# A gated delta-net block with a routed FFN on one core: output's roots on VectorE, a shorter root for m, v scaled behind x's norm, q transposed by halves, VectorE's loop one step earlier

## What is computed

```
x = x + attn(layernorm(x))
    h  = rms_norm(x);  q, k = l2norm(silu(h Wq)), l2norm(silu(h Wk));  v = silu(h Wv)       # 8 heads of 128
    per token and head:  S = alpha S;  S += k (beta (v - k S));  o = q S / sqrt(128)
    h  = (rms_norm(o) * o_norm_w * silu(h Wg)) Wo;   x = x + h
    m  = rms_norm(x);   y = relu(m W_fc)^2 W_proj;   result x + y
x = x + ffn(layernorm(x))
    logits = x gate_W^T;  pi = 20 sinkhorn rounds;  the two best of 8 experts per token
    y = sum over the two of pi * (silu(x Wgate) * (x Wup)) Wdown
```

## Time and profile before

| | us |
|---|---|
| median of 3 runs (lowest, highest) | 2452.66 (2448.92, 2453.04) |
| the profiled execution, its own time | 2450.82 |
| its span, first to last instruction | 2449.0 |
| busy PE, PEld, DVE, ACT, POOL | 2167.5, 1907.3, 1810.2, 1076.7, 763.9 |

### The profile page before, as it was taken

The page is one execution under the profiler, slowest core; times in us unless marked ns, Lnnn a source line. Parts: engine busy times, 40 slices in busy tenths (PEclk is TensorE's granted clock), DMA queues, the critical chain, the costliest instruction groups (busy, mean ns, idle before and its releaser), DMA issues.

```text
span 2449.0 us, 51704 instructions
## 1 busy us (share of the span) xinstructions
PE 2167.5 (89%) x16283; PEld 1907.3 (78%) x16283; DVE 1810.2 (74%) x4317; ACT 1076.7 (44%) x2288; POOL 763.9 (31%) x1559
## 2 busy tenths in 40 slices
PE   4579999999999999999999998632599999999998
PEld 4468888888888888888888887521599999999887
DVE  6678887888888888888888787377666676666553
ACT  2334444444444444444444443221555555555442
POOL 0113332332333333323323333000234444434332
PEclk9789999999999999999999999855799999999999
DMA  5312212212122122122121221000345445445340
GB/s 189 104 33 48 42 36 48 41 36 52 37 43 48 36 46 42 36 49 41 36 54 35 44 46 25 7 7 2 135 158 175 154 162 182 148 155 175 123 129 18
DMA packets 307850, 182.26 MB, mean 74 GB/s; under 512 B 244716, under 2 KB 286064, under 8 KB 298512
## 3 DMA queue, kind: packets, MB, share of 16 engines
q1 hardware_dynamic: 255184, 149.21, 21.7%
q0 software_dynamic: 11280, 29.31, 4.2%
q10 hardware_dynamic: 41264, 2.51, 1.1%
HBM read 150.23 MB, written 32.51 MB: 75 GB/s over the span
## 4 chain that ended last, share of the span: by engine, by line
PE 43%; DVE 29%; issue 10%; DMA 6%; POOL 5%; ACT 3%; SPq 2%; POOLq 1%; DVEq 1%; ACTq 0%
PE ps_inva L744 9%; PE ps_invb L744 9%; PE ps_back L744 8%; PE ps_back L1984 4%; DMA xi<-xy_d 3%; PE ps_back L2001 3%; DVE state L1661 3%; DVE o_s L1682 2%; PE ps_front L1884 2%; DVE xi L1613 2%; DVE xi L1607 2%; DVE yi L1606 2%; DMA xy_d<-lane_x 2%; DVE yi L1612 1%; PE ps_back L1974 1%
## 5 line engine op out<-in xcount | busy, mean ns | idle before, releaser
L614 DVE TENSOR_TENSOR w_lo<-w_raw,w_hi 128x512 fp32r<-128x512 f32 x288 | 190.1, 688 | 3.9
L744 PE MATMUL ps_back<-w_hi,eh_hi 128*128 128x256 f32 x624 | 180.1, 289 | 3.2 <-DVE eh_lo L624 3.2
L744 PE MATMUL ps_back<-w_lo,eh_hi 128*128 128x256 f32 x624 | 176.5, 283 | 0.0
L744 PE MATMUL ps_back<-w_hi,eh_lo 128*128 128x256 f32 x624 | 176.4, 283 | 0.1
L698 ACT ACTIVATE w_hi<-w_raw 128x512 fp32r<-128x512 f32 x288 | 169.5, 626 | 0.0
L710 ACT ACTIVATE sact<-ps_inva 128x512 f32<-128x512 f32 (+1 forms) x96 | 49.8, 519 | 239.5 <-PE ps_inva L744 213.3
L1940 PE MATMUL ps_back<-state,kqT_t 128*128 128x128 f32 x1024 | 132.7, 282 | 24.0 <-DVE r_s L1641 22.7
L1940 PEld LDWEIGHTS ps_back<-state,kqT_t 128*128 128x128 f32 x1024 | 125.4, 193 | 32.5 <-DVE r_s L1641 26.5
L1283 ACT ACTIVATE v_s<-ps_front 128x512 f32<-128x512 f32 x64 | 38.1, 595 | 230.0 <-PE ps_front L744 230.0
L1283 ACT ACTIVATE g_s<-ps_front 128x512 f32<-128x512 f32 x64 | 38.3, 599 | 226.1 <-PE ps_front L744 214.8
L744 PE MATMUL ps_inva<-xT_hi,w_hi 128*128 128x512 f32 (+1 forms) x384 | 135.5, 353 | 1.9 <-DVE xT_lo L619 1.7
(11 more groups left out here) (385 smaller groups left out, 6743.0 us busy)
## 6 DMA issues: line engine op xcount, KB each, us to landing
w_raw<-L_ffn_W_gate_dram SPq DMA_DIRECT2D x24, 1024.0 KB
w_raw<-L_ffn_W_up_dram SPq DMA_DIRECT2D x24, 1024.0 KB
w_raw<-L_ffn_W_down_dram SPq DMA_DIRECT2D x24, 1024.0 KB
dT<-alphaT_d SPq DMA_DIRECT2D x32, 512.0 KB, 3.7
x_all<-L_attn_x_dram SPq DMA_DIRECT2D x4, 1024.0 KB, 10.0
hTr<-hT_d SPq DMA_DIRECT2D x32, 128.0 KB, 3.7
lt_d<-aP SPq DMA_DIRECT2D x256, 8.0 KB, 1.5
xi<-low_d SPq DMA_DIRECT2D x32, 128.0 KB
```

The lines of the kernel that those rows point to most:

```text
L614: V.tensor_tensor(piece(w_lo[p], m).bitcast(F32R), piece(w_raw, m), piece(w_hi[p], m), ALU.subtract).then_inc(split[n], 1)
L744: ins = MM(out_, w[a].bitcast(F32R), x[b].bitcast(F32R), start=start and n == 0, stop=stop and n == 2)
```

## The change

- **o's root**: POOL keeps three operations (`o_squares`) and writes the value into `root_v[:, 1, :]`, signalled by `ov_ready`. DVE's `k_root` puts k's value into `root_v[:, 0, :]`, waits for `ov_ready`, and takes both roots in the same ten instructions, 128x16 instead of 128x8. `tail_o` then runs from inside `k_root`, ahead of sqk, nb1 and nbh, which come after it. In step 31, which has no front, DVE takes o's root by itself.
- **m's root**: the mean and epsilon are folded into the sum of squares (scale and start value of L1693), and the last factor into m's scaling on DVE (L1699, now with a second, constant factor). POOL's chain has 7 operations instead of 9. x's root keeps its 9.
- **v**: POOL waits for `xf_ready` of tile t-1 ahead of `scaled_v`.
- **q**: PE does the first half of `state_q`, the transposes of q's first half, the second half, the transposes of the second half.
- **DVE's loop** holds steps 1 to 28.
- The memsets of ones and state and the first semaphore counts move from POOL to DVE, at the start; the last tile's code loses one operation.

```diff
-                roots(os_[:, 1, :], or_[:, 0, :], or_[:, 1, :], o_pool, n + 3, or_ready)
+                pool.tensor_tensor(root_v[:, 1, :], os_[:, 1, :], qe[:, :], ALU.add).then_inc(ov_ready, 1)
...
-                n = N_ROW * t + 1
-                link(pool.tensor_scalar(mrow_v[:, 1:2], mrow_v[:, 0:1], 1.0 / D, RMS_EPS, ALU.mult, ALU.add), m_pool, n)
-                row_root(mrow_v[:, 1:2], mrow_r[:, 0:1], mrow_r[:, 1:2], m_pool, n, mr_ready)
+                newton(mrow_v[:, 0:1], mrow_r[:, 0:1], mrow_r[:, 1:2], m_pool, N_M * t).then_inc(mr_ready, 1)
...
                 if tail:
                     x_root(t - 1)
+                    if more:
+                        pool.wait_ge(xf_ready, t)
                 if more:
                     scaled_v(f)
...
-            def k_root(f, q):
+            def k_root(f, q, t=None):
...
+                    dve.wait_ge(ov_ready, t + 1)
+                    dve.sem_inc(dve_turn, 1)
+                    root(ch, root_v[:, :, :], root_r[:, :, :], root_a[:, :, :])
+                    tail_o(t)
+                rk = root_r[:, 0, :]
+                ch.mark(V.tensor_tensor(sqk[:, :], root_v[:, 0, :], rk, ALU.mult))
...
-            step(1, 1, True, True, True)
-            with dve.Fori(1, PAIRS) as i:
+            with dve.Fori(0, PAIRS - 1) as i:
                 for p in range(2):
-                    step(2 * i + p, p, True, True, True)
+                    step(2 * i + p + 1, 1 - p, True, True, True)
+            step(TILES - 3, 1, True, True, True)
...
-                state_q(t)
-                if more:
-                    transposes(f, FU_TQ, q_s)
+                for g in range(G):
+                    state_q(t, [g])
+                    if more:
+                        transposes(f, FU_TQ, q_s, [g])
```

More of the change, by code:

```diff
@@ L148, in program @@
         msc = sb("msc", [P, 2])
-        ssk, nv, na, rn, sqk, nb1, dbh = (sb(n, [P, H]) for n in ("ssk", "nv", "na", "rn", "sqk", "nb1", "dbh"))
+        ssk, sqk, nb1, dbh = (sb(n, [P, H]) for n in ("ssk", "sqk", "nb1", "dbh"))
+        root_v, root_r, root_a = (sb(n, [P, 2, H]) for n in ("root_v", "root_r", "root_a"))
         nbh = sb("nbh", [P, 2, H])
@@ L1147, in first_root, with newton @@
                 link(pool.tensor_scalar(r.bitcast(I32), v.bitcast(I32), -0.5, ROOT_MAGIC, ALU.mult, ALU.add), chain, n)
[L1149 to L1162, removed]
+            def newton(v, r, a, chain, n):
                 first_root(v, r, chain, n + 1)
@@ L1168, in row_root @@
                     link(pool.tensor_scalar(a, r, r, v, ALU.mult, ALU.mult), chain, m + 1)
-                    link(pool.tensor_scalar(r, a, -3.0 * c * c, r, ALU.add, ALU.mult), chain, m + 2)
+                    last = pool.tensor_scalar(r, a, -3.0 * c * c, r, ALU.add, ALU.mult)
+                    if k < 2:
+                        link(last, chain, m + 2)
                     c *= -2.0 * c * c
-                pool.tensor_scalar(r, r, 1.0 / c, None, ALU.mult).then_inc(ready, 1)
+                assert c == NEWTON
+                return last
             def front_scalars_free(f):
@@ L1494, in aggregate @@
                 return ins
+            V.memset(ones[:, :], 1.0).then_inc(consts, 1)
+            V.memset(state[:, :], 0.0).then_inc(consts, 1)
+            for s in front_evac + back_evac:
+                dve.sem_inc(s, 1)
+            dve.sem_inc(ba_ready, 2)
+            dve.sem_inc(pre_tr, 4)
+            for s in [x1_stored, xf_stored] + hT_stored:
+                dve.sem_inc(s, 16)
             for n in range(XPARTS):
@@ L1737, in step @@
                 if more:
-                    k_root(f, q)
-                if tail:
+                    k_root(f, q, t - 1 if tail else None)
+                elif tail:
+                    ch = Chain(dve, o_dve)
+                    dve.wait_ge(ov_ready, t)
+                    dve.sem_inc(dve_turn, 1)
+                    root(ch, root_v[:, 1, :], root_r[:, 1, :], root_a[:, 1, :])
                     tail_o(t - 1)
@@ L1806, in _ @@
             dve.wait_ge(mv_ready, TILES)
[L1807 to L1808 removed]
+            root(ch, mrow_v[:, 0:1], mrow_r[:, 0:1], mrow_r[:, 1:2])
             dve.sem_inc(mr_ready, 1)
[L1810 removed]
+            tail_m(TILES - 1, 1.0)
             tail_fc(TILES - 1)
@@ L1870, in project, with transposes @@
                 last.then_inc(filled, 1)
-            def transposes(f, u0, src):
-                for n in range(G):
+            def transposes(f, u0, src, halves=range(G)):
+                for n in halves:
                     ps, filled = front_bank(f, u0 + n)
@@ L1945, in state_k, with state_q @@
                     heads(t, BU_KS + g, g, lambda c: kqT[:, c, 0, :], lambda c: cols(state, c))
-            def state_q(t):
-                for g in range(G):
+            def state_q(t, halves=range(G)):
+                for g in halves:
                     heads(t, BU_QS + g, g, lambda c: kqT[:, c, 1, :], lambda c: cols(state, c))
```

52 lines of the change are left out of this document (20 added, 32 removed).

## The result

The changed kernel takes **2387.9 us** (median of 4 runs, 2386.5 to 2388.1), the kernel before 2452.85 (2448.9 to 2456.1). The ratio is 0.9735, with a 95% interval of 0.9718 to 0.9752. The profiled execution took 2388.1 us, with a span of 2386.3.

A forecast was written before the change was run, and what follows sets the result against it. PE's busy time was taken as the bound, its idle time as what can be won. Savings of 2.07 us a pair, 29.0 in 14 pairs, 32.2 with the ends, off 2450.8 gave 2418 us, range 2404 to 2434.

The forecast's parts named there:

- the one on the loop: DVE's jump moves from ahead of even steps to ahead of odd ones; no change in its 1.73 us cost taken.
- The 1.73: DVE's issue wait after its loop jump, between os and ssk: 1.73 us, bounds 1.73 either way.
- Rival 4: At the loop jump: DVE's instructions come later because four other engines fetch then; 2442 to 2467 us, chance 0.05.
- where I had 3.2: Start and end of the kernel, outside the 14 pairs: 3.2 us won together, mostly at step 31 and step 29.
- The 0.55: DVE's copy L1614 beside POOL's v: held 0.55 us, leaving 0.36 of the 0.91 won at x's norm.
- Rival 1: DVE's copy L1614 beside POOL's v isn't held: 0.91 instead of 0.36 reaches r_s, 2411 us, chance 0.32.
- POOL wasn't first: Case behind x's norm: v's scaling gets ahead of L1612, DVE held 2.2 us, 2459 us, chance 0.06.
- x's blocks are not what PE waits for next: Case at the small inverse: x's blocks from DRAM (margin 0.6) hold PE, 2432 us, chance 0.14.
- the 0.75 that I had for the end: Step 31, where DVE waits 2.75 us for o's root: its replacement ends about 0.75 us sooner.
- The 0.30: PE's wait for m's scaled rows: 0.30 us a step goes, as m's root comes 0.74 earlier.
- the sum 0.42 meets the 0.41 that DVE is earlier: Step 16: PE's waits for kqT (0.25) and o's rows (0.17) go together; 0.41 us taken.
- A step can't fall much below 42.9: Floor of a step from PE's busy time, 42.89 us; only PE's idle time, 3.67 us a pair, can be won.

The follow-up runs named there:

- e12: The kernel before with 35 empty semaphore increments ahead of DVE's first wait, loop still over steps 2 to 29: 2429.35 us, ratio 0.9901.
- e3: The kernel before with 163 empty semaphore increments ahead of DVE's first wait, loop still over steps 2 to 29: 2429.75 us, ratio 0.9908.
- e4: The changed kernel with 93 empty semaphore increments ahead of DVE's first wait: 2417.0 us, ratio 0.9854.
- e6: The changed kernel with 60 empty semaphore increments ahead of DVE's first wait: 2417.9 us, ratio 0.9848.
- e1: The kernel before with DVE's loop moved to steps 1 to 28 and nothing else: 2503.1 us, ratio 1.0203.
- e2: The changed kernel with DVE's loop moved back over steps 2 to 29: 2436.2 us, ratio 0.9929.
- e7: The changed kernel without POOL's wait for x's norm (`xf_ready`) ahead of v's scaling: 2403.0 us, ratio 0.9783.
- e9: The changed kernel with all of o's root back on POOL (15 operations) and o's scaling behind k's scalars: 2400.4 us, ratio 0.9779.
- e10: The changed kernel with m's root in nine operations on POOL again: 2398.55 us, ratio 0.9780.
- e8: The changed kernel with `state_q` whole ahead of all of q's transposes, as before: 2388.8 us, ratio 0.9735.
- e11: The changed kernel with POOL's v waiting for the pairs' inverse instead of x's norm, `msc` copy moved ahead of x's norm: 2384.3 us, ratio 0.9726.
- e5: The changed kernel with 48 empty semaphore increments ahead of DVE's first wait: 2386.5 us, ratio 0.9727.

## Why the prediction missed, and where it held

**The step that failed is the one on the loop**: "I take no change, as the mechanics of a step are the same for both parities." The 1.73 was read rightly as the price of a jump, but that both parities do the same work says nothing about whether it stays, and no case in the list of rivals took it away. The bound of 1.73 in the kernel's favour, 14 times, would have given 2394, outside the range that I then stated. The price is a property of where the loop's code lies. Moved to steps 1 to 28 in the changed kernel, the loop begins at instruction 333 and touches three pages, and the wait is gone. That is worth some 23 us on the kernel before (e12, e3) and 29 to 30 on the changed one (e4, e6); that it is worth more there because the other parts had used up the slack beside it is argued, not shown. The page showed the clue: q14, 0.76 MB of instructions, for a program whose loop should be fetched once. I hadn't read that row. Rival 4 had the mechanism by its name (instructions that come late) but only in the direction of worse, and e1 shows that side too: 50 us slower. It needs no other engine's jump for it, though: the wait at the jump is about as long where the jumps meet (1.88 to 1.90 us in e1, e4 and e6) as where they don't (1.76 before, 1.96 in e2). What makes e1 slow is the second page, and the clock that falls behind it.

**The rest was right in sum, in part by luck.** With the loop again in four pages (e4, e6) the changed kernel takes 2417.0 and 2417.9, against 2418 forecast, and its pair is 2.0 us shorter than before, against 2.07. But the step without the jump gives 1.27 and 1.13 there, where I had 1.0, and the one with it 0.74 and 0.89, where I had 1.07: two misses that cancel. Without fetching on either side the parts are worth 2429.4 - 2387.9 = 41.5, and undone one by one 15.1 + 12.5 + 10.7 + 0.9 = 39.2: nearly additive. The pairs say the same with less scatter:

| kernel | mean of 13 pairs, us | 14 times the difference from the changed one |
|---|---|---|
| before | 89.75 | 58.7 |
| before, padded 35 | 87.95 | 33.6 |
| changed | 85.55 | |
| v not behind x (e7) | 86.49 | 13.1 |
| o's root on POOL (e9) | 86.18 | 8.7 |
| m's root of nine (e10) | 86.49 | 13.1 |
| q whole (e8) | 85.49 | -0.9 |
| v behind the pairs (e11) | 85.43 | -1.7 |

The four parts make 34.0 of 33.6. The 8 us between that and the 41.5 lie outside the pairs, where I had 3.2.

Single terms:

- *v behind x's norm*: x's norm at 0.41 in every step, v's recorded 2.48, DVE first at the two-input operation, the reductions beside v at 1.22 as ever, the copy held. All as taken, but the copy is held for 0.32 and not for 0.55. The 0.55 was wrong as a sum too: 3.1 - 2.4 + 0.14 - 0.22 + 0.2, as I wrote it, is 0.82, by which v's move would have been worth 0.09 a step and the forecast 2422. In the trace v ends 2.88 behind x's norm, and the copy 0.08 behind v. Rival 1, where it isn't held at all, is refuted; e11 shows that the price reaches PE for a few hundredths a step. The Trainium skill (SBUF — State Buffer, "Who interferes with whom") has VectorE and GpSimd share a pair of ports under an exclusive lock: the first to start keeps it, copies, tensor_scalar and operations with two SBUF inputs can ask for it, a reduce never does. The trace agrees for the four of them named here. No rival of this part came: POOL wasn't first, and x's blocks are not what PE waits for next (one wait of 1.6 us for x<-x_d in all the steps).
- *o's root*: undone it costs 12.5 us (e9), of which the pairs have 8.7, 0.31 a step; I had 0.41 for it and kqT together in the step with the jump. In step 31 o_s starts at 1463.19, 0.03 behind the root's last operation, with no wait for POOL. PE's wait for it there is 0.67 us, where it was 1.02 before and is 0.80 in e9, so little of the 0.75 that I had for the end shows.
- *m's root*: I took 0.30 a step and 0.74 at the end, 9.1 us; PE's waits differ by 9.1 us between e10 and the changed kernel, the time by 10.7, the pairs by 13.1, which is 0.47 a step. The 0.30 was too small.
- *q by halves*: the wait goes, as said, and nothing is gained by it (0.9, e8), because o_s and aP come no sooner. My sum had it in one term with o, "the sum 0.42 meets the 0.41 that DVE is earlier", which is the same thing: DVE's part pays, q's only makes room.
- *"A step can't fall much below 42.9"* failed as well. Steps are at 42.75 with PE busy 42.27 to 42.37, 0.6 less than the 42.89 of the earlier trace rows. e7 shows how such a floor comes out too high: there 0.27 of 0.49 us of delay stood in the busy time. This is also how a step without jump could fall by 1.2 where I had taken 1.0 of 1.08.

Open is what makes the 5.3 us outside the pairs where 3.2 were forecast, with ends that scatter by 10 us, and whether the fourth page held is the one behind the loop. Where the offset of 65 comes from wasn't tried.

## What to carry to other kernels

When an engine shows an "issue" wait behind a loop's jump, look at its instruction queue's packets: if they grow with the iterations, the loop is being fetched anew, and whether it is depends on its place, so try a few dozen idle instructions ahead of it (35 of them took some 23 us off the kernel before; of the 65 us of the whole change, more than a third is of this kind). A change that adds or removes instructions ahead of such a loop moves its place too, so part of the difference measured may have nothing to do with the edit; pad both versions into the same state before you judge the edit. And a wait that is taken away at one place counts only when the chain behind it comes sooner: q's halves took 7 us of waits away and gained nothing.

## What the runs showed of the hardware that I had not expected

- VectorE fetches instructions in packets of 8192 bytes. A loop of 316 to 319 instructions was kept in the four kernels of the table in which it touched three such pages (28 to 30 packets in the whole run) and fetched again in the five in which it touched four: five packets and 1.8 to 2.0 us of standing still in each iteration, and 2.5 us more where a page ends 2 instructions behind the loop's head.
- A wait of PE of 4.1 to 4.7 us in every second step (e1) is followed each time by a stretch at 1.2 GHz, in which 16 matmuls take up to 3.78 us instead of 2.19; after the waits of 1.6 to 1.9 us of the kernel before they take 2.19.
- Twelve idle instructions ahead of the loop made 31 us (e5 and e6), 163 of them made the kernel before 23 us faster (e3).
- A 128x64 copy on VectorE is held beside POOL's 1.90 us operation: 539 ns instead of 217, while the 128x1024 reductions there stay at 1.22 us.
- PE's busy time isn't its work alone: the same 721 matmuls of a pair of steps count as 85.93 us in the kernel before, 85.18 in e7 and 84.64 in the changed one, with the granted clock at 1.00 in all.
